# Moving ScalarE's norm chain by one slot in a software-pipelined local-attention stage

## The chip, the cores and the metric

One program on one core of one Trainium2 chip. The metric is device time in microseconds of that core; smaller is better.

## The reference, cut to what matters

The model is a stack of four pairs of cross-attention and feed-forward on x of shape (4, 256, 128). The first feed-forward slot holds six *local layers*, and these fill most of the time. Each local layer is, for every one of the 4 batch rows and for 16 heads of 64:

```python
qkv = shift_tokens(x) @ Wqkv;  q, k, v = split(qkv)
q = l2norm(q) * q_scale;  k = l2norm(k) * k_scale      # t / max(|t|, 1e-12) per head
q, k = rotary(q), rotary(k)
sim = einsum('bhwie,bhwje->bhwij', q, look(k)) * 8      # windows of 32, each with the one before it
out = softmax(mask(sim)) @ look(v);  x = out @ Wo + x
x = ffn(shift_tokens(x)) + x                            # LayerNorm, W1, a * gelu(gate), W2
```

The change concerns `l2norm`: the sums of squares of a unit's query and key per head, and from them 1/|t|.

## The kernel before, in words

All of it is float32. The six local layers are cut into 96 *units*: 6 layers x 4 batch rows x 2 blocks of 128 tokens x 2 halves of 8 heads (`unit_of`). The loop over `LOCAL_SLOTS` (96) is written once for every engine (`pe_local`, `act_local`, `dve_local`, `pool_local`, and the unit loop of `sync_program`), each with its own hand-written order of calls inside a slot. The engines meet only through semaphores that count units. A slot s works on several units at once, by the lags `TURN, SCORE, SOFT, VALUE, OUT = 2, 3, 4, 5, 6`. The LayerNorm and feed-forward of a finished batch row (`ended(slot, lag)`) are spread over slots by lags from 10 to 15, so there are four kinds of slot, by s mod 4.

**TensorE in slot s**, in order (line of the matmul): query of unit s (L721), transposes of the rotated query of s-2 (L750), output projection of s-6 (L822), with s mod 4 = 0 the gate products (L662, L663), value of s (L741), key of s (L730), with s mod 4 = 2 the LayerNorm centring (L255), transposes of the weights of s-5 (L791), scores of s-3 (L780, 64 small matmuls), weighted values of s-5 (L807, 64 small matmuls), feed-forward parts (L265, L671, L679 to L688), transposes of the rotated key of s-2 (L758), and with s mod 4 = 2 the last feed-forward product (L697). `pe_weighted` (L807) waits first for `p_kept` of unit s-5. `pe_turn_query` waits for `k_kept` of the unit before, as both use one bank.

**ScalarE in slot s** (`act_local`): with s mod 4 = 3 the LayerNorm Ln and Exp (L270, L272); squares of the query of s (L1875); Exp of the scores of s-4 (L1920); last gate (L1958); copy of the turned query of s-2 (L1896); copy of the value of s (L1889); squares of the key of s (L1882); copy of the turned weights of s-5 (L1927, sets `p_kept`); gates (L1951, L1952), LayerNorm squares (L260), Gelu with its two table loads (L1965 to L1967, s mod 4 = 1); copy of the turned key of s-2 (L1905); copy of the weighted values of s-5 (L1935); and last `act_norm` of unit s (L1911, L1913, L1915: Relu, Ln and Exp over 128x16, each waiting for the one before), which waits for `summed` of unit s.

**VectorE in slot s** (`dve_local`): residual of s-6 (L2899, L2900), the three rotary products of the query of s (L2858 to L2860, after its squares), sum and reciprocal of the weights of s-4 (L2888, L2890), the three products of the key (after its squares), mask and maximum of s-3 (L2880, L2882), and last `dve_norm`: the two sums of squares of unit s (L2867, L2868), which set `summed`.

**GpSimd in slot s** (`pool_local`): normalise the weights of s-5 (L4001), add of the key of s-1 (L3975), multiply the query of s-1 by the norms (L3982, waits for `norm_done` of s-1), with s mod 4 = 3 a LayerNorm scale (L4007), add of the query of s (L3970), lower the scores of s-3 by their maximum (L3995), multiply the key of s-1 by the norms (L3989), and in the last slot of a layer the rotary tables of the next (L643).

The norms of unit s lie in one of four buffers (`local_small[u % 4]`), the sums in the same place. The queue of SyncE carries the value windows and the weights and has no norm in it.

```python
def pe_weighted(e, s, m, u):
    e.wait_ge(s["p_kept"], u + 1)
def pool_norm_query(e, s, m, u):
    e.wait_ge(s["norm_done"], u + 1)
```

Of the kernel before, what the change touches and what calls it, by code (L numbers as in the profile page):

```python
# [212 lines left out]
UNITS = DEPTH * B * LAYER_UNITS  # L213
# [16 lines left out]
def ended(slot, lag):  # L230
    lb, rest = divmod(slot - lag, LAYER_UNITS)
    return lb if rest == 0 and 0 <= lb < DEPTH * B else None
# [14 lines left out]
def ln_views(buf):  # L247
    return buf[:, 0:N], buf[:, N:2 * N]
# [9 lines left out]
def act_ln_square(e, s, i, views, bank):  # L258
    e.wait_ge(s["ln_centred"], i + 1)
    e.activation(views[0], bank[:, 0:N], ACT.Square).then_inc(s["ln_squared"], 1)  # L260
# [7 lines left out]
def act_ln_rstd(e, s, i, views, bank, eps):  # L268
    e.wait_ge(s["ln_var"], i + 1)
    e.activation(views[1], bank[:, N:2 * N], ACT.Ln, bias=eps).then_inc(s["ln_logged"], 1)  # L270
    e.wait_ge(s["ln_logged"], i + 1)
    e.activation(views[1], views[1], ACT.Exp, scale=-0.5).then_inc(s["ln_rstd"], 1)  # L272
# [434 lines left out]
def live(u):  # L707
    return 0 <= u < UNITS
# [1162 lines left out]
def act_square_query(e, s, m, u):  # L1871
    e.wait_ge(s["q_made"], u + 1)
    if u >= 2:
        e.wait_ge(s["summed"], u - 1)
    e.activation(m.sq_q[u % 2], m.bank[QB], ACT.Square).then_inc(s["q_squared"], 1)  # L1875


def act_square_key(e, s, m, u):
    e.wait_ge(s["k_made"], u + 1)
    if u >= 2:  # L1880
        e.wait_ge(s["summed"], u - 1)
    e.activation(m.sq_k[u % 2], m.bank[KB], ACT.Square).then_inc(s["k_squared"], 1)  # L1882


def act_value(e, s, m, u):
    e.wait_ge(s["v_made"], u + 1)
    if u >= 4:
        e.wait_ge(s["v64_even"] if u % 2 == 0 else s["v64_odd"], windows_loaded(u - 2))
    e.activation(m.vt[u % 4], m.bank[VB], ACT.Copy).then_inc(s["v_kept"], 1)  # L1889


def act_query(e, s, m, u):
    e.wait_ge(s["q_turned"], u + 1)
    if u >= 2:
        e.wait_ge(s["scored"], u - 1)
    e.activation(m.qT[u % 2], m.bank[TB], ACT.Copy).then_inc(s["q_kept"], 1)  # L1896


def act_key(e, s, m, u):
    lb, stage, b, t, half = unit_of(u)  # L1900
    kT = split(m.kT[(lb % 2) * 2 + half], UP)[:, :, PAD + t * P:PAD + (t + 1) * P]
    if u == 0:
        e.wait_ge(s["zeros_ready"], 1)
    e.wait_ge(s["k_turned"], u + 1)
    e.activation(kT, split(m.bank[TB], UP), ACT.Copy).then_inc(s["k_kept"], 1)  # L1905


def act_norm(e, s, m, u):
    norm = m.local_small[u % 4][:, 0:16]
    e.wait_ge(s["summed"], u + 1)  # L1910
    e.activation(norm, norm, ACT.Relu, bias=m.minus_floor).then_inc(s["norm_logged"], 1)  # L1911
    e.wait_ge(s["norm_logged"], 2 * u + 1)
    e.activation(norm, norm, ACT.Ln, bias=m.floor).then_inc(s["norm_logged"], 1)  # L1913
    e.wait_ge(s["norm_logged"], 2 * u + 2)
    e.activation(norm, norm, ACT.Exp, scale=-0.5).then_inc(s["norm_done"], 1)  # L1915


def act_exp(e, s, m, u):
    e.wait_ge(s["lowered"], u + 1)
    e.activation(m.e[u % ES], m.e[u % ES], ACT.Exp).then_inc(s["exped"], 1)  # L1920


def act_weights(e, s, m, u):
    e.wait_ge(s["p_turned"], u + 1)
    if u >= 2:
        e.wait_ge(s["o_made"], u - 1)
    e.activation(m.pT[u % 2], m.bank[PB], ACT.Copy).then_inc(s["p_kept"], 1)  # L1927


def act_out(e, s, m, u):  # L1930
    e.wait_ge(s["o_made"], u + 1)
    if u >= 2:
        e.wait_ge(s["y_made"], u - 1)
    outs = split(m.banks[:, VB * BANK:(PB + 1) * BANK], 2)[:, :, 0:N]
    e.activation(split(m.oT[u % 2], 2), outs, ACT.Copy).then_inc(s["o_kept"], 1)  # L1935


def act_ln_start(e, s, m, lb):
    act_ln_square(e, s, ln_of_local(lb), ln_views(m.ln_local), m.bank[FB])


def act_ln_end(e, s, m, lb):
    act_ln_rstd(e, s, ln_of_local(lb), ln_views(m.ln_local), m.bank[FB], m.eps)


def act_gates(e, s, m, lb):
    b1 = m.W(home_of(lb)[0], "b1")
    e.wait_ge(s["gate01_made"], lb + 1)
    if lb:
        e.wait_ge(s["a2_done"], lb)  # L1950
    e.activation(m.gate[:, 0:N], m.bank[FB][:, 0:N], ACT.Identity, bias=b1[:, 3:4])  # L1951
    e.activation(m.gate[:, N:2 * N], m.bank[FB][:, N:2 * N], ACT.Identity, bias=b1[:, 4:5]).then_inc(s["gate01_kept"], 1)  # L1952


def act_last_gate(e, s, m, lb):
    rows = FFC[2][1]
    e.wait_ge(s["gate2_made"], lb + 1)
    e.activation(m.gate[0:rows, 2 * N:3 * N], m.bank[FB][0:rows, 0:N], ACT.Identity,  # L1958
                 bias=m.W(home_of(lb)[0], "b1")[0:rows, 5:6]).then_inc(s["gate2_kept"], 1)


def act_gelu(e, s, m, lb):
    rows = FFC[2][1]
    e.wait_ge(s["gate2_kept"], lb + 1)
    e.activation(m.gate[:, 0:2 * N], m.gate[:, 0:2 * N], ACT.Gelu)  # L1965
    e.activation(m.gate[0:rows, 2 * N:3 * N], m.gate[0:rows, 2 * N:3 * N], ACT.Gelu).then_inc(s["gelued"], 1)
    e.preload_act_table_set("natural_log_exp_and_others")  # L1967


def act_local(e, s, m):  # L1970
    for slot in range(LOCAL_SLOTS):
        if ended(slot, RSTD) is not None:
            act_ln_end(e, s, m, ended(slot, RSTD))
        if live(slot):
            act_square_query(e, s, m, slot)
        if live(slot - SOFT):
            act_exp(e, s, m, slot - SOFT)
        if ended(slot, KEEP2) is not None:
            act_last_gate(e, s, m, ended(slot, KEEP2))
        if live(slot - TURN):  # L1980
            act_query(e, s, m, slot - TURN)
        if live(slot):
            act_value(e, s, m, slot)
            act_square_key(e, s, m, slot)
        if live(slot - VALUE):
            act_weights(e, s, m, slot - VALUE)
        if ended(slot, KEEP) is not None:
            act_gates(e, s, m, ended(slot, KEEP))
        if ended(slot, SQUARE) is not None:
            act_ln_start(e, s, m, ended(slot, SQUARE))  # L1990
        if ended(slot, GELU) is not None:
            act_gelu(e, s, m, ended(slot, GELU))
        if live(slot - TURN):
            act_key(e, s, m, slot - TURN)
        if live(slot - VALUE):
            act_out(e, s, m, slot - VALUE)
        if live(slot):
            act_norm(e, s, m, slot)
        if slot == 0:
            act_ln_square(e, s, 2 * B - 1, ln_views(m.ln_local), m.bank[FB])  # L2000
        if slot == 1:
            act_ln_rstd(e, s, 2 * B - 1, ln_views(m.ln_local), m.bank[FB], m.eps)
# [2431 lines left out]
def build(nc, x_in, ctx_in, gates_in, const_in, packs_in, out):  # L4434
    with ExitStack() as stack:
# [10 lines left out]
        @block.scalar  # L4446
        def _(e):
            act_cross0(e, s, m)
            act_local(e, s, m)
            act_drain(e, s, m)  # L4450
# [147 lines left out]
```

## Time and profile before

| | us |
|---|---|
| three runs | 1290.18, 1287.36, 1283.38 |
| their median | 1287.36 |
| the profiled execution's own time | 1283.86 |
| its span, first to last instruction | 1282.1 |
| local stage: first L721 to last L721 | 177.2 to 970.8 |
| busy over the span: PE, DVE, ACT, POOL | 95%, 77%, 73%, 61% |

The profiled execution is some 3.5 us below the median of the three. The span is 1.8 us shorter than its time. The stage of the 96 slots takes from 177 to about 978 us, some 8.35 us a slot. The mean granted TensorE clock over the span is 0.990 of full speed. A row of a timeline gives start, duration, engine and line; a bracket at its end is the engine's idle time before it and what ended that. ScalarE, VectorE and TensorE overlap the end of one instruction with the start of the next, so an instruction's cost in a full queue is the distance from its start to the next start, not its duration.

### The profile page before, as it was taken

What the parts mean: (1) busy time and instruction counts of PE and PEld (TensorE: products, weight loads), DVE (VectorE), ACT (ScalarE), POOL (GpSimd) and SP (SyncE); (2) the same over time, 40 slices, a digit from 0 to 9 for tenths busy, and PEclk for the clock granted to TensorE, in tenths of its full rate; (3) what the DMA queues carried; (4) which work ended last, traced back from release to release, by engine and by line L of the source; (5) the groups of instructions that cost most, each with busy time, mean ns of one, the idle gap of its engine ahead of it and who ended that gap; (6) DMA issues with size and microseconds to landing.
All of it is one profiled execution on the core that took longest, in us unless ns stands there. A gap on an engine that the chain in (4) does not pass through costs nothing.

```text
span 1282.1 us, 44796 instructions
## 1 busy us (share of the span) xinstructions
PE 1214.4 (95%) x17900; PEld 870.4 (68%) x17900; DVE 986.0 (77%) x2513; ACT 937.0 (73%) x2310; POOL 786.2 (61%) x805
## 2 busy tenths in 40 slices
PE   7999988999999999999999999999999999999997
PEld 5777745666766677667777677667777877777553
DVE  4666668887887888878888788888888655778677
ACT  6777765677776777777777777777777768788891
POOL 3444447878876877778778777887776102635100
PEclk9999999999999999999999999999999989999998
DMA  5000032222223322342225222432232002213000
GB/s 213 1 2 1 2 116 72 68 63 57 62 62 101 100 64 62 81 125 59 59 62 146 60 61 63 123 84 65 63 81 60 2 1 87 81 35 91 2 1 17
DMA packets 71743, 81.89 MB, mean 64 GB/s; under 512 B 15456, under 2 KB 63584, under 8 KB 71024
## 3 DMA queue, kind: packets, MB, share of 16 engines
q1 hardware_dynamic: 71536, 79.03, 22.4%
q8 instruction: 143, 2.34, 0.8%
q14 instruction: 64, 0.52, 0.1%
HBM read 31.22 MB, written 0.56 MB: 25 GB/s over the span
## 4 chain that ended last, share of the span: by engine, by line
PE 50%; ACT 18%; DVE 17%; issue 10%; POOL 5%; DMA 1%; SPq 0%; ACTq 0%; DVEq 0%; POOLq 0%
PE banks L822 3%; PE banks L807 3%; PE banks L390 2%; PE banks L730 2%; PE banks L741 2%; PE banks L721 2%; ACT arena L2183 2%; PE banks L1142 2%; DVE arena L2858 2%; PE banks L750 2%; PE banks L1136 2%; PE banks L419 2%; DVE arena L2859 2%; DVE small L2867 2%; PE banks L404 2%
## 5 line engine op out<-in xcount | busy, mean ns | idle before, releaser
L3995 POOL TENSOR_TENSOR arena<-arena,small 128x512 f32<-128x512 f32 x93 | 97.1, 1044 | 139.2 <-DVE small L2882 139.2
L1905 ACT ACTIVATE arena<-banks 128x512 f32<-128x512 f32 x94 | 56.2, 598 | 142.3 <-PE banks L758 142.1
L2858 DVE TENSOR_TENSOR arena<-banks,rotary 128x512 f32<-128x512 f32 x192 | 131.6, 685 | 26.8 <-ACT arena L1875 15.9
L3970 POOL TENSOR_TENSOR arena<-arena 128x512 f32<-128x512 f32 x96 | 122.9, 1280 | 30.4 <-DVE arena L2860 30.3
L807 PE MATMUL banks<-arena 64*64 64x32 f32 x5824 | 107.3, 220 | 17.8 <-issue 11.5
L3975 POOL TENSOR_TENSOR arena<-arena 128x512 f32<-128x512 f32 x95 | 121.5, 1279 | 0.2 <-DVE arena L2860 0.2
L606 POOL TENSOR_TENSOR arena<-arena,small 128x512 f32<-128x512 f32 x64 | 66.6, 1041 | 89.0 <-DVE small L533 89.0
L807 PEld LDWEIGHTS banks<-arena 64*64 64x64 f32 x5824 | 95.5, 134 | 29.3 <-issue 12.5
L721 PE MATMUL banks<-slot,z 128*128 128x512 f32 x192 | 100.2, 604 | 3.0 <-DVE arena L2860 1.9
L3982 POOL TENSOR_TENSOR arena<-arena,small 128x512 f32<-128x512 f32 x95 | 99.7, 1049 | 1.3 <-ACT small L1915 1.3
L3989 POOL TENSOR_TENSOR arena<-arena,small 128x512 f32<-128x512 f32 x95 | 99.2, 1044 | 0.0
L741 PE MATMUL banks<-slot,z 128*128 128x512 f32 x192 | 99.0, 598 | 0.0
L730 PE MATMUL banks<-slot,z 128*128 128x512 f32 x192 | 98.0, 592 | 0.0
L822 PE MATMUL banks<-arena,slot 128*128 128x128 f32 x720 | 97.4, 278 | 0.0
L4001 POOL TENSOR_TENSOR arena<-arena,small 128x512 f32<-128x512 f32 x91 | 95.0, 1044 | 0.0
L460 ACT ACTIVATE arena<-arena,small 128x256 f32<-128x256 f32 x128 | 63.7, 500 | 39.7 <-DVE small L565 39.7
L750 PEld LDWEIGHTS banks<-constants,arena 128*128 128x128 f32 x376 | 42.3, 142 | 69.8 <-issue 69.0
L822 PEld LDWEIGHTS banks<-arena,slot 128*128 128x128 f32 x720 | 87.3, 191 | 0.5
L2899 DVE TENSOR_TENSOR z<-z,banks 64x128 f32<-64x128 f32 x90 | 25.0, 277 | 77.4 <-PE banks L822 77.3
L780 PE MATMUL banks<-arena 64*32 64x64 f32 x5952 | 80.9, 224 | 0.5 <-issue 0.5
L2860 DVE TENSOR_TENSOR arena<-banks,rotary 128x256 f32<-128x256 f32 x192 | 79.3, 413 | 0.0
L2859 DVE TENSOR_TENSOR arena<-banks,rotary 128x256 f32<-128x256 f32 x192 | 79.3, 413 | 0.0
(403 smaller groups left out, 3366.3 us busy)
## 6 DMA issues: line engine op xcount, KB each, us to landing
arena<-arena SPq DMA_DIRECT2D x576, 64.0 KB
slot<-in_pack_dram SPq DMA_DIRECT2D x28, 339.5 KB, 3.6
arena<-arena SPq DMA_DIRECT2D x288, 32.0 KB
slot<-in_pack_dram SPq DMA_DIRECT2D x2, 2713.5 KB, 9.1
slot<-in_pack_dram SPq DMA_DIRECT2D x1, 2693.5 KB
slot<-in_pack_dram SPq DMA_DIRECT2D x1, 2316.5 KB
arena<-gate_store SPq DMA_DIRECT2D x8, 256.0 KB, 4.0
slot<-in_pack_dram SPq DMA_DIRECT2D x4, 337.0 KB, 4.3
```

Source lines behind the costliest of these rows:

```text
L721: e.matmul(m.bank[QB], m.zs[b][:, t * P:(t + 1) * P], m.W(stage, "Wqkv")[:, half * BANK:(half + 1) * BANK], start=True, stop=True, skip_gr ...
L730: e.matmul(m.bank[KB], m.zs[b][:, t * P:(t + 1) * P], m.W(stage, "Wqkv")[:, at:at + BANK], start=True, stop=True, skip_group_check=True).t ...
L741: e.matmul(m.bank[VB], m.zs[b][:, t * P:(t + 1) * P], m.W(stage, "Wqkv")[:, at:at + BANK], start=True, stop=True, skip_group_check=True).t ...
L807: made = e.matmul(m.bank[PB if x else VB][y * DH:(y + 1) * DH, to:to + WINDOW], v[rows, i, k, :], pT[rows, at:at + WINDOW], start=True, st ...
L822: made = e.matmul(m.bank[S0][:, N:N + P], wo[:, c * D:(c + 1) * D], oT[:, k * P:(k + 1) * P], start=(k == 0), stop=(k == UP - 1), skip_gro ...
L2858: e.tensor_tensor(rot, made, cos, ALU.mult)
L2859: e.tensor_tensor(sinp[:, :, 0:mid], made[:, :, mid:DH], sin[:, :, 0:mid], ALU.mult)
L3970: e.tensor_tensor(m.rot_q[u % ROTS], m.rot_q[u % ROTS], m.sin_q[u % 2], ALU.add).then_inc(s["q_added"], 1)
L3975: e.tensor_tensor(m.rot_k[u % ROTS], m.rot_k[u % ROTS], m.sin_k[u % 2], ALU.add).then_inc(s["k_added"], 1)
L3982: e.tensor_tensor(q, q, stretch(m.local_small[u % 4][:, 0:UH], DH), ALU.mult).then_inc(s["q_rotated"], 1)
L3989: e.tensor_tensor(k, k, stretch(m.local_small[u % 4][:, UH:2 * UH], DH), ALU.mult).then_inc(s["k_rotated"], 1)
L3995: e.tensor_tensor(p, p, stretch(m.local_small[u % 4][:, 16:24], SPAN), ALU.subtract).then_inc(s["lowered"], 1)
```

## The change

`act_norm` of a unit moves from the end of its own slot to the middle of the next slot, right behind the squares of that slot's key and ahead of the copy of the turned weights. Slot 95 has it in both places, for unit 94 in the middle and for unit 95 at the end. No instruction, wait or buffer is added or removed.

```diff
@@ -1982,6 +1982,8 @@
         if live(slot):
             act_value(e, s, m, slot)
             act_square_key(e, s, m, slot)
+            if slot:
+                act_norm(e, s, m, slot - 1)
         if live(slot - VALUE):
             act_weights(e, s, m, slot - VALUE)
         if ended(slot, KEEP) is not None:
@@ -1994,7 +1996,7 @@
             act_key(e, s, m, slot - TURN)
         if live(slot - VALUE):
             act_out(e, s, m, slot - VALUE)
-        if live(slot):
+        if slot == UNITS - 1:
             act_norm(e, s, m, slot)
         if slot == 0:
             act_ln_square(e, s, 2 * B - 1, ln_views(m.ln_local), m.bank[FB])
```

## Rows read from the trace of the kernel before

**Rows 1.** Busy time of PE, PEld, DVE, ACT, POOL: slots 59-62; whole stage

```profile
664.61:698.57 33.96, 32.89 (x640) 23.86 (x639) 28.23 (x63) 25.34 (x54) 26.77 (x26) 1.00 0.44 122
...
sum 793.00, PE 756.22 PEld 541.19 DVE 656.48 ACT 580.76 POOL 629.39; mean PE 94.53 PEld 67.65 DVE 82.06 ACT 72.59 POOL 78.67
```

**Rows 2.** Waits in the stage, 177 to 970 us: total, times, longest

```profile
ACT arena L1905 <- PE banks L758: 139.7, 73, 4.3
...
ACT small L1911 <- DVE small L2868: 42.1, 50, 3.5
...
PE banks L807 <- issue: 11.5, 15, 2.1
...
PE banks L807 <- ACT arena L1927: 6.0, 19, 0.6
```

**Rows 3.** Timeline of slot 59 (s mod 4 = 3)

```profile
664.28 0.68 DVE L2868 TENSOR_REDUCE small<-arena 128x8 f32<-128x512 f32 x1
...
664.99 0.31 ACT L1911 ACTIVATE small<-small,eps 128x16 f32<-128x16 f32 x1 [0.39 <-DVE small L2868]
...
665.67 0.21 ACT L1915 ACTIVATE small<-small 128x16 f32<-128x16 f32 x1
665.79 0.46 ACT L270 ACTIVATE arena<-banks,eps 128x256 f32<-128x256 f32 x1
...
667.66 1.02 PE L730 MATMUL banks<-slot,z 128*128 128x512 f32 x2
...
668.08 1.05 POOL L3982 TENSOR_TENSOR arena<-arena,small 128x512 f32<-128x512 f32 x1
...
668.52 0.60 PE L791 MATMUL banks<-constants,arena 128*128 128x128 f32 x4
...
668.72 0.60 ACT L1882 ACTIVATE arena<-banks 128x512 f32<-128x512 f32 x1
...
669.05 0.86 PE L780 MATMUL banks<-arena 64*32 64x64 f32 x64
...
669.21 0.59 ACT L1927 ACTIVATE arena<-banks 128x512 f32<-128x512 f32 x1
...
669.86 1.14 PE L807 MATMUL banks<-arena 64*64 64x32 f32 x64
```

**Rows 4.** Timeline of slot 69 (s mod 4 = 1)

```profile
752.98 1.02 PE L730 MATMUL banks<-slot,z 128*128 128x512 f32 x2
...
754.27 0.60 ACT L1882 ACTIVATE arena<-banks 128x512 f32<-128x512 f32 x1
...
755.40 1.14 PE L807 MATMUL banks<-arena 64*64 64x32 f32 x64 [0.18 <-ACT arena L1927]
```

**Rows 5.** Timeline of slot 62 (s mod 4 = 2)

```profile
692.58 1.02 PE L730 MATMUL banks<-slot,z 128*128 128x512 f32 x2
...
694.50 0.60 ACT L1927 ACTIVATE arena<-banks 128x512 f32<-128x512 f32 x1 [0.27 <-PE banks L791]
...
695.23 1.13 PE L807 MATMUL banks<-arena 64*64 64x32 f32 x64
```

**Rows 6.** Timeline of the fill: norms of units 0, 4; slot 6

```profile
183.20 0.31 ACT L1911 ACTIVATE small<-small,eps 128x16 f32<-128x16 f32 x1 [2.67 <-DVE small L2868]
...
209.13 0.31 ACT L1911 ACTIVATE small<-small,eps 128x16 f32<-128x16 f32 x1 [3.54 <-DVE small L2868]
...
215.46 1.02 PE L721 MATMUL banks<-slot,z 128*128 128x512 f32 x2
```

**Rows 7.** Timeline of TensorE: a wait in slot 16, a stall in slot 28

```profile
300.37 0.66 PE L791 MATMUL banks<-constants,arena 128*128 128x128 f32 x4 [1.12 <-POOL arena L4001]
...
405.53 0.54 PE L807 MATMUL banks<-arena 64*64 64x32 f32 x22 [2.06 <-issue]
```

**Rows 8.** Busy times, clock (before the last two): slot 16; behind slot 28

```profile
299.00:304.00 5.00, 3.88 (x140) 3.13 (x140) 4.58 (x10) 2.23 (x6) 4.79 (x6) 1.00 0.26 63
...
407.30:410.50 3.20, 3.20 (x14) 2.01 (x13) 0.00 (x0) 2.84 (x8) 2.77 (x3) 0.59 0.77 237
```

## The prediction

> **What bounds the kernel now.** I read the busy times by stretch first, then the waits of the local stage, then the timelines of single slots. The busy times show an almost full TensorE: 32.89 of 33.96 us in four typical slots, 756 of 793 us in the stage, with ScalarE at 25.3 and GpSimd at 26.8 us of the same 33.96 [rows 1]. So TensorE's 37 us of idle time are all that an edit of the other engines can win there. The waits show why the edit looks attractive: in 50 slots ScalarE stood before the norms for the sums of squares, 42.1 us in all [rows 2]. But its largest wait, 139.7 us, is for TensorE's turned keys, so time saved ahead of that is mostly waited again. The reader is to look next at what TensorE waits for: on ScalarE's copy of the weights (L1927) it waited 6.0 us in 19 slots, the figure to watch, as that copy is what the edit puts the norms in front of.
>
> The timeline of slot 59 shows how tight it is [rows 3]. TensorE's key product (L730) ends at 668.68, ScalarE squares the key from 668.72, copies the weights from 669.21 to 669.80, and TensorE begins the weighted values (L807) at 669.86. Meanwhile TensorE has the turning of the weights and the scores, from 668.52 on; the scores' last start falls just before 669.86. The cover is used up to 0.06 us: nothing can go between the squares and the weights' copy without TensorE waiting for it.
>
> **The change, part by part.** *Price of a norm in ScalarE's queue.* Start to start from the Relu (664.99) to the instruction behind the Exp (665.79) it is 0.80 us [rows 3]. The count of instructions stays, so nothing is paid for work, only for place. The Trainium skill ("ScalarE: Activation LUTs", Rules for kernel authors) budgets about 0.3 us per ACTIVATE and 0.83 ns per element, an estimate of 0.94 us for three over 16 elements; by it the steady sum would be about 12 us larger. The row's start-to-start time is for this very triple and I use it alone.
>
> *Norms of s-1 between squares and weights' copy.* The sums of unit s-1 end with the slot before (664.96 for a slot whose key squares come at 668.72, [rows 3]), so the norms start at once. From L730's end to L807's start it will take 0.04 + 0.49 + 0.80 + 0.59 + 0.06 = 1.98 us in every slot, as the squares cannot start before L730 ends on the same TensorE. What it takes now differs by kind of slot. s mod 4 = 3: 1.18 us, so +0.80 [rows 3]. s mod 4 = 0: no work stands between L730 and L791 there either, +0.80. s mod 4 = 1: L730 ends at 754.00, L807 starts at 755.40; the squares came 0.23 us late, because ScalarE had entered the slot behind its norms; this lateness goes, +0.58 [rows 4]. s mod 4 = 2: a LayerNorm product stands before the turning of the weights, the copy waited 0.27 us for it, and the gap is 693.60 to 695.23, 1.63 us, so +0.35 [rows 5]. Four slots pay 2.53 us. Weights are copied in slots 5 to 95; the 90 slots from 6 on make 22.5 fours: **+57 us**.
>
> *Exceptions among these.* In slots 7 to 11 the squares come 0.4 to 0.7 us late today, more than in slot 69: -2. In the slots that follow GpSimd's tables, as slot 16, TensorE waits 1.12 us for the normalised weights [rows 7]; the norms fit in that wait and cost nothing: three such slots, and part of it in two more, -3. In slot 95 TensorE waits for something else anyway: -1. **Steady part +51 us.**
>
> *Norms away from the end of the slot.* There ScalarE no longer stands for the sums and enters the next slot up to 0.8 us earlier, or more. In the steady part this gives only the 0.23 us counted above: queries, values and keys arrive when TensorE makes them, and TensorE is late by then. Behind the Gelu with its table loads (s mod 4 = 1) TensorE waits for the turned key; both ends of that chain move with L807, so the wait stays. While the pipeline fills it gives more: in slots 0 to 4 ScalarE stood five times before the norms, 2.67 us at the first and 3.54 at the last [rows 6], and the squares of the next query, its products and the next slot's query came behind. I walked these slots with the new order and the durations of the rows: now GpSimd's multiply by the norms sets them, and slot 6 starts near 209 and not at 215.46: **-6 us**. Its bounds are 0 (another wait takes each one's place) and about -15 (five waits of some 3 us all gone).
>
> *GpSimd.* Its multiply of the query (L3982), at 668.08 in slot 59, will wait for norms that end near 668.72 + 0.49 + 0.68 + 0.21 = 670.10, 2.0 us later. Behind it queue a LayerNorm scale, an add, the lowering of the scores, the other multiply, the normalising of the next weights. GpSimd works 26.8 us in four slots that become 36.5 long, so 2.4 us a slot are idle [rows 1]. Walked through, the next weights are normalised near 676.2 and TensorE turns them near 677.1 at the new pace: 1.0 us of slack, cost 0. The bounds: 0, and 1 us a slot of one kind in four, +24 us. In the slot behind the tables the slack is negative, as today.
>
> *VectorE and queues.* The query's products come earlier, the key's as before. SyncE's queue has no norm in it and no DMA moves: 0. *The stalls called "issue"*, in the midst of L807, total 11.5 us in 15 slots [rows 2]. A TensorE that has just waited may have its next instructions at hand, which would remove up to all of it; but such stalls also stand in slots with a wait before L807, so I count 0 and keep -12 as an end.
>
> **Sum.** +57 - 6 - 6 = +45 us. Against the profiled execution's own 1283.86 this is 1328.9; that execution is 3.5 us below the median of the three runs, against which it is 1332.4. I give 1330.
>
> **The rivals.** *Faster, because the norm wait set the period.* The loop is sums, norms, squares of the next query, its products. If L807 did not really hang on L1927, the 42.1 us of waiting before the norms would fall out, as far as TensorE's 37 us of idle time allow: 1283.9 - 37 = 1247. For it speaks that the chain of waits of the page runs over DVE and ACT for a third of the span; against it, that TensorE hardly idles and L807 starts 0.06 us behind the copy. It would decide only if the copy had 0.8 us of slack. *No difference:* if TensorE's scores really end 0.8 us later than the modelled ends say, the delay would hide and the time stay near 1284. *The instruction stalls vanish:* 1330 - 12 = 1318. *GpSimd becomes the bound,* behind its later multiply: 1330 + 24 = 1354.
>
> *The clock falls.* Behind the 2.06 us stall in slot 28 [rows 7] the granted clock was 0.59 for 3.2 us, that is, partly 1.2 instead of 2.4 GHz; behind the 1.12 us wait of slot 16 it stayed at 1.00 [rows 8]. The new waits are 0.35 to 0.8 us, shorter than both, so I expect no fall. If one came per four slots at slot 28's price, 3.2 x 0.41 = 1.3 us, it would add 24 x 1.3 = 31 us: 1361. The Trainium skill ("TensorE: Matmul & The Clock Gate", A second HAM failure mode) says that frequent short idle times between groups of matmuls can make the clock swing; by that rule the edit would cost more than its waits, while slot 16's row so far speaks against it.
>
> **How the numbers follow.** The forecast 0.78; stalls vanish 0.08; GpSimd bound 0.04; clock 0.05; faster 0.03; no difference 0.02. About 0.5% is what a measurement of this kernel can tell from no change. Faster 0.03, same 0.02, slower 0.95. The range takes in the fill's bounds (-9 and +6 around 1330), the vanished stalls (1318) and a few us of slack lost on GpSimd: 1315 to 1346.
>
> **What would show it.** Right: in every steady slot L1882, L1911, L1913, L1915, L1927 in one row, L807 starting 0.06 us behind L1927's end with a wait on it of 0.35 to 0.8 us, some 50 to 57 us over the stage in the waits where there were 6.0; the wait of L1911 for L2868 gone; slot 6 starting near 209; stage longer by about 45 us, everything after unchanged. Wrong: L807 without a wait; TensorE waiting for L3982 or L4001 in ordinary slots; a granted clock below 1.00 in typical slots; or slot 6 still near 215.

## The result, and the profile after

The changed kernel takes 1318.69 us (median of six runs, 1316.82 to 1321.41) against 1285.12 us (the kernel before, six runs, 1281.63 to 1290.18): ratio 1.026, 95% interval 1.024 to 1.028. It is slower by some 34 us; 45 were forecast, and the time lies inside the stated range. The profiled execution took 1317.78 us, with a span of 1316.0.

The waits of the stage after, 177 to 1000 us: each row has what waited and for what, then the total in us, how often, and the longest. A wait called `issue` is one for which the profile shows no semaphore. `L3984` is GpSimd's multiply of the query (L3982 before; lines behind the edit shift by two), the other lines are those of before.

```profile
POOL arena L3984 <- ACT small L1915: 178.8, 88, 3.2
ACT arena L1905 <- PE banks L758: 125.5, 68, 3.4
...
ACT arena L1889 <- PE banks L741: 62.1, 92, 1.5
PE banks L807 <- ACT arena L1927: 53.3, 85, 1.0
...
PE banks L750 <- POOL arena L3984: 4.2, 4, 2.2
PE banks L791 <- POOL arena L4003: 3.8, 6, 0.8
...
PE banks L807 <- issue: 2.9, 4, 1.6
```

Read against [rows 2], three things moved. ScalarE's wait for the sums of squares, 42.1 us in the stage before, is not among them any more. TensorE's wait at L807 for the weights' copy rose from 6.0 to 53.3 us. And the stalls called issue in L807 fell from 11.5 to 2.9 us. ScalarE did not save its 42.1 us: it now stands 62.1 us for TensorE's value product (L741), which was 3.5 us before. The largest wait, GpSimd's for the norms, is new and costs nothing in the ordinary slots: TensorE's wait for GpSimd at L791 is 3.8 us, no more than before:

```profile
PE banks L791 <- POOL arena L4001: 4.5, 4, 1.5
...
ACT arena L1889 <- PE banks L741: 3.5, 8, 0.7
```

Its four waits at L750, 4.2 us, all lie in slots 2 to 5, while the pipeline fills.

The timeline of slot 59 after, the same slot as in [rows 3] (start, duration, engine and line; the bracket is idle time before it):

```profile
683.54 1.02 PE L730 MATMUL banks<-slot,z 128*128 128x512 f32 x2
...
684.60 0.60 ACT L1882 ACTIVATE arena<-banks 128x512 f32<-128x512 f32 x1 [0.26 <-PE banks L730]
...
684.93 0.86 PE L780 MATMUL banks<-arena 64*32 64x64 f32 x64
685.09 0.30 ACT L1911 ACTIVATE small<-small,eps 128x16 f32<-128x16 f32 x1
685.42 0.31 ACT L1913 ACTIVATE small<-small,eps 128x16 f32<-128x16 f32 x1
...
685.76 0.22 ACT L1915 ACTIVATE small<-small 128x16 f32<-128x16 f32 x1
...
685.88 0.58 ACT L1927 ACTIVATE arena<-banks 128x512 f32<-128x512 f32 x1
686.05 1.04 POOL L3984 TENSOR_TENSOR arena<-arena,small 128x512 f32<-128x512 f32 x1 [2.41 <-ACT small L1915]
...
686.52 1.14 PE L807 MATMUL banks<-arena 64*64 64x32 f32 x64 [0.73 <-ACT arena L1927]
```

L730 ends at 684.56, L807 starts at 686.52: 1.96 us, where 1.98 was worked out and 1.18 stood before. The norms' place in ScalarE's queue, 685.09 to 685.88, is 0.79 us wide. The scores of L780, which used to end just as the copy did, now end 0.73 us before L807 can start. In the other kinds of slot:

```profile
774.53 1.02 PE L730 MATMUL banks<-slot,z 128*128 128x512 f32 x2
...
777.51 1.13 PE L807 MATMUL banks<-arena 64*64 64x32 f32 x64 [0.73 <-ACT arena L1927]
```

```profile
710.51 1.02 PE L730 MATMUL banks<-slot,z 128*128 128x512 f32 x2
...
713.48 0.73 PE L807 MATMUL banks<-arena 64*64 64x32 f32 x36 [0.29 <-ACT arena L1927]
```

The first is slot 69 (1.96 us from L730's end, 1.40 before), the second slot 62 (1.95 us, 1.63 before). One chain now sets these kinds of slot alike. Slots 59 to 62, and the whole stage (us, then busy PE, PEld, DVE, ACT, POOL, clock, DMA, GB/s):

```profile
680.49:716.82 36.33, 33.04 (x639) 23.82 (x638) 28.56 (x62) 25.77 (x55) 26.68 (x26) 1.00 0.41 113
...
177.00:1004.30 827.30, 755.18 (x14506) 537.84 (x14507) 661.71 (x1434) 589.08 (x1241) 630.37 (x620) 1.00 0.30 77
```

The four slots are 2.37 us longer than before (36.33 against 33.96), where 2.53 was worked out. TensorE does the same work, 755.18 us against 756.22 [rows 1], in a stage some 34 us longer. Its granted clock is 1.00 on average over the stage. The stage's beginning:

```profile
203.47 1.11 PE L750 MATMUL banks<-constants,arena 128*128 128x128 f32 x4 [2.25 <-POOL arena L3984]
...
211.71 0.59 PE L721 MATMUL banks<-slot,z 128*128 128x512 f32 x1
```

Slot 6 starts at 211.71 and not at 215.46 [rows 6]: the fill gave 3.8 us (4.0 counted from each kernel's own first L721, at 177.5 and 177.2).

### The profile page after: what moved, and what is told of

Read it like the earlier page. It is cut to its first block, busy times and chain, and to the rows that moved or that the text cites. A ratio compares the mean times of both kernels' runs of the same rounds, so it can differ in the third digit from the quotient of the medians.

```text
span 1316.0 us, 44796 instructions
## 1 busy us (share of the span) xinstructions
PE 1214.0 (92%) x17900; PEld 866.4 (66%) x17900; DVE 990.4 (75%) x2513; ACT 945.3 (72%) x2310; POOL 786.0 (60%) x805
## 4 chain that ended last, share of the span: by engine, by line
PE 66%; ACT 21%; issue 4%; DVE 4%; POOL 3%; SPq 1%; DMA 1%; ACTq 0%; DVEq 0%; POOLq 0%
PE banks L822 6%; PE banks L807 6%; PE banks L730 6%; PE banks L741 6%; PE banks L721 4%; ACT arena L1882 4%; ACT arena L1927 4%; PE banks L750 3%; PE banks L758 2%; PE banks L390 2%; ACT small L1913 2%; PE banks L697 2%; ACT L1965 2%; PE banks L1142 2%; PE banks L1136 2%
## 5 line engine op out<-in xcount | busy, mean ns | idle before, releaser
L3984 POOL TENSOR_TENSOR arena<-arena,small 128x512 f32<-128x512 f32 x95 | 99.2, 1044 | 184.0 <-ACT small L1915 184.0
L807 PE MATMUL banks<-arena 64*64 64x32 f32 x5824 | 104.5, 220 | 57.1 <-ACT arena L1927 54.1
L1905 ACT ACTIVATE arena<-banks 128x512 f32<-128x512 f32 x94 | 56.1, 597 | 129.6 <-PE banks L758 129.4
L807 PEld LDWEIGHTS banks<-arena 64*64 64x64 f32 x5824 | 93.9, 134 | 72.0 <-ACT arena L1927 68.2
L3997 POOL TENSOR_TENSOR arena<-arena,small 128x512 f32<-128x512 f32 x93 | 97.2, 1046 | 12.1 <-DVE small L2884 11.9
L1889 ACT ACTIVATE arena<-banks 128x512 f32<-128x512 f32 x96 | 57.4, 598 | 64.5 <-PE banks L741 62.7
L721 PE MATMUL banks<-slot,z 128*128 128x512 f32 x192 | 98.5, 594 | 0.9 <-DVE arena L2862 0.9
L741 PE MATMUL banks<-slot,z 128*128 128x512 f32 x192 | 99.1, 598 | 0.0
L730 PE MATMUL banks<-slot,z 128*128 128x512 f32 x192 | 98.4, 594 | 0.0
L750 PEld LDWEIGHTS banks<-constants,arena 128*128 128x128 f32 x376 | 41.3, 141 | 76.4 <-issue 68.8
L780 PE MATMUL banks<-arena 64*32 64x64 f32 x5952 | 80.1, 224 | 0.2 <-issue 0.2
L2862 DVE TENSOR_TENSOR arena<-banks,rotary 128x256 f32<-128x256 f32 x192 | 79.6, 414 | 0.0
```

Of the source, the lines that this page charges most:

```text
L721: e.matmul(m.bank[QB], m.zs[b][:, t * P:(t + 1) * P], m.W(stage, "Wqkv")[:, half * BANK:(half + 1) * BANK], start=True, stop=True, skip_gr ...
L730: e.matmul(m.bank[KB], m.zs[b][:, t * P:(t + 1) * P], m.W(stage, "Wqkv")[:, at:at + BANK], start=True, stop=True, skip_group_check=True).t ...
L741: e.matmul(m.bank[VB], m.zs[b][:, t * P:(t + 1) * P], m.W(stage, "Wqkv")[:, at:at + BANK], start=True, stop=True, skip_group_check=True).t ...
L807: made = e.matmul(m.bank[PB if x else VB][y * DH:(y + 1) * DH, to:to + WINDOW], v[rows, i, k, :], pT[rows, at:at + WINDOW], start=True, st ...
L3984: e.tensor_tensor(q, q, stretch(m.local_small[u % 4][:, 0:UH], DH), ALU.mult).then_inc(s["q_rotated"], 1)
L3997: e.tensor_tensor(p, p, stretch(m.local_small[u % 4][:, 16:24], SPAN), ALU.subtract).then_inc(s["lowered"], 1)
```

## The experiments

All ratios are to the kernel before, run on the same chip in the same session. Its median differs between the sessions, so the ratios are to be compared, and not the times across sessions; each interval is that of the ratio. Every kernel was profiled once.

| kernel | median us (runs) | before, same session | ratio, 95% interval | L807 waits for copy, us | L807 issue, us |
|---|---|---|---|---|---|
| before | 1285.12 (6) | | 1 | 6.0 | 11.5 |
| the change | 1318.69 (6) | 1285.12 | 1.026 (1.024 to 1.028) | 53.3 | 2.9 |
| norms behind the weights' copy | 1309.42 (4) | 1283.89 | 1.019 (1.014 to 1.024) | none | 12.1 |
| norms ahead of the value's copy | 1276.21 (8) | 1283.89 | 0.994 (0.991 to 0.997) | 0.4 | 13.1 |
| the same again | 1277.12 (6) | 1287.72 | 0.990 (0.988 to 0.993) | 0.4 | 12.0 |
| norms ahead of the Exp | 1276.63 (6) | 1287.72 | 0.992 (0.989 to 0.995) | 0.4 | 11.2 |
| norms ahead of the key's squares | 1292.17 (10) | 1283.89 | 1.005 (1.003 to 1.007) | 22.8 | 3.5 |
| before + three activations | 1322.94 (4) | 1283.89 | 1.030 (1.025 to 1.035) | 54.7 | 0.9 |
| before + one activation | 1289.56 (10) | 1287.94 | 1.001 (0.998 to 1.003) | 8.3 | 8.7 |
| before + three, at the turned key | 1332.54 (4) | 1287.94 | 1.034 (1.031 to 1.037) | 1.1 (at L750: 52.8) | 11.7 |
| change from unit 6 on | 1319.60 (4) | 1287.94 | 1.024 (1.021 to 1.027) | 51.9 | 2.9 |
| change up to unit 4 | 1279.83 (6) | 1287.94 | 0.993 (0.990 to 0.996) | 6.2 | 12.0 |

The two columns at the right are the rows "PE banks L807" of each kernel's waits, 177 to 1000 us; "none" means that there is no such row. They list single waits of some 0.2 us and more.

**Norms behind the weights' copy.** The edit to the changed kernel:

```diff
-            if slot:
-                act_norm(e, s, m, slot - 1)
         if live(slot - VALUE):
             act_weights(e, s, m, slot - VALUE)
+        if slot:
+            act_norm(e, s, m, slot - 1)
```

> Norms of s-1 one place later than in the change: behind the copy of the weights (L1927), ahead of gates and Gelu. Theory (TensorE hangs on the weights' copy, the norms' 0.80 us in front of it are the whole loss): the wait of L807 for that copy falls to nearly nothing, 49 us come back. Instead the key's copy behind the Gelu comes 0.8 us later in one slot of four and L750 waits for it, 22 x 0.8 = +18 us; lateness of the squares in one slot of four goes, -5; fill -4; the stalls called issue return to some 11 us. Time about 1285 + 18 - 5 - 4 = 1294. Rival (what costs is that the norms come a slot later at all, so that GpSimd's multiply is late): the time stays near 1319 or rises, since the norms here end 0.5 us later still.

Measured: 1309.42 us. The wait at L807 is gone, as the theory says, so it is the copy of the weights that the norms must not stand before. But the time is 15 us above what I expected. Its waits show most of why:

```profile
PEld banks L791 <- POOL arena L4003: 39.2, 45, 2.9
...
PE banks L750 <- ACT arena L1905: 18.2, 17, 1.1
...
PE banks L791 <- POOL arena L4003: 11.9, 10, 2.1
...
PE banks L671 <- ACT arena L1952: 6.6, 19, 0.6
```

Beside the wait for L1905 behind the Gelu that I had named (18.2 us, 5.1 before), TensorE waits at L671 for the gates, which in slots with s mod 4 = 0 now stand behind the norms, and at L791 for GpSimd's normalising: 11.9 us against 4.5. Most of this stands in the fill (1.86 us) and in four slots behind GpSimd's tables (some 2.1 us each). The 45 waits of the weight load there (PEld, 39.2 us) show that the slack is used up in ordinary slots as well. Further, the granted clock was some 0.5 in three stretches of this trace's stage (0.52 at 310.0 to 313.4, 0.50 at 689.0 to 695.8 and at 726.6 to 730.0); in the changed kernel such a fall stands only in the fill. So the rival, late norms through GpSimd, is real at this place, if small; at the place of the change the ordinary slots do not show it.

**Norms ahead of the value's copy.**

```diff
         if live(slot):
+            if slot:
+                act_norm(e, s, m, slot - 1)
             act_value(e, s, m, slot)
             act_square_key(e, s, m, slot)
-            if slot:
-                act_norm(e, s, m, slot - 1)
```

> Norms of s-1 ahead of the copy of the value of s, where ScalarE stands 0.6 us a slot for TensorE's value product in the changed kernel. Theory: neither squares of the key nor weights' copy are delayed, and ScalarE no longer stands for the sums at the end of a slot: L807 waits below 5 us in all, lateness of the squares goes (22 x 0.23 = -5 us), fill -4 to -6: about 1275, faster than both. Rival (the later norms themselves cost, through GpSimd or through ScalarE entering the value late): not faster than 1285; a rival half-way is that Exp and last gate push the value, and with it the squares, by up to 0.4 us in some slots: about 1290.

> The kernel with the norms of s-1 ahead of the copy of the value of s once more, in more rounds and beside the one with the norms ahead of the Exp. Theory: fill -4 and lateness of the squares in one slot of four -5, with the stalls called issue as before: ratio 0.992 to 0.996. Rival (the first comparison was luck of the instruction stalls): 0.997 to 1.000.

Measured: ratio 0.994 and 0.990, both intervals below 1. It is faster than both kernels: 8 and 11 us below the kernel before, a little more than I expected in the second session. The timeline of its slot 59:

```profile
659.82 0.31 ACT L1911 ACTIVATE small<-small,eps 128x16 f32<-128x16 f32 x1
...
660.32 1.02 PE L730 MATMUL banks<-slot,z 128*128 128x512 f32 x2
...
660.62 0.58 ACT L1889 ACTIVATE arena<-banks 128x512 f32<-128x512 f32 x1
...
661.37 0.60 ACT L1882 ACTIVATE arena<-banks 128x512 f32<-128x512 f32 x1 [0.17 <-PE banks L730]
...
661.87 0.59 ACT L1927 ACTIVATE arena<-banks 128x512 f32<-128x512 f32 x1
...
662.51 1.13 PE L807 MATMUL banks<-arena 64*64 64x32 f32 x64
```

The same three activations, also a slot late, stand where ScalarE would wait for TensorE's value product. From L730's end (661.34) to L807 it is 1.17 us again. "A slot later" costs next to nothing (TensorE's wait at L791 is 6.2 us against 4.5); the place is what costs. The gain is in the trace too: the 6.0 us of waiting at L807 are down to 0.4, and slot 6 starts at 212.50 and not at 215.46, together some 8 us.

**Norms ahead of the Exp.** The same two lines directly behind `act_square_query`.

> Norms of s-1 one place further ahead than in front of the value: directly behind the squares of the query of s, ahead of the Exp of the scores, for which ScalarE stood 11 us in 21 slots with the norms in front of the value. Theory (all places ahead of the value product are free): no wait of L807 for the weights' copy above the 5 us of the kernel with the norms ahead of the value, same time as that within 4 us, ratio to before 0.992 to 0.997. Rival: the Exp 0.8 us later makes VectorE's sums of the weights and with them the normalising late, so L791 waits for L4003: slower than the kernel before by 0.5% or more.

Measured: 0.992, at the lower edge of what the theory says, and the rival is out; its interval overlaps that of the place ahead of the value, so the two are not told apart.

**Norms ahead of the key's squares.** The two lines between `act_value` and `act_square_key`.

> Norms of s-1 between the value's copy and the squares of the key. ScalarE has some 0.37 us to spare there before the key product is done, so theory says the squares come 0.43 us late and the gap from L730's end to L807's start is 1.61 us in each kind of slot, not 1.98: +0.43, +0.43, +0.2, 0 against before by kind, 1.07 per four slots = +24 us; fill -4, stalls called issue about -5: about 1300. Rival (any place in the middle of the slot costs the whole 0.80): 1315 to 1320.

Measured: 1.005, 1292.17 us; 1300 was expected and the rival's 1315 is excluded. TensorE waits 22.8 us at L807. That is 17 us more than before, where the working had 24 more; and the issue stalls fell by 8.0 us to 3.5, where I had allowed 5. These two more than cover the 8 us by which I was too high.

**Three more activations in the kernel before**, nothing moved. They write spare columns and no output depends on them:

```diff
+def act_extra(e, s, m, u):
+    spare = m.local_small[u % 4][:, 40:56]
+    e.activation(spare, m.ident[:, 0:16], ACT.Relu, bias=m.minus_floor).then_inc(s["mask_ready"], 1)
+    e.wait_ge(s["mask_ready"], 3 * u + 3)
+    e.activation(spare, spare, ACT.Ln, bias=m.floor).then_inc(s["mask_ready"], 1)
+    e.wait_ge(s["mask_ready"], 3 * u + 4)
+    e.activation(spare, spare, ACT.Exp, scale=-0.5).then_inc(s["mask_ready"], 1)
...
             act_square_key(e, s, m, slot)
+            act_extra(e, s, m, slot)
```

> The kernel before with three further activations of the norms' size and kinds on spare columns, each waiting for the one before, right behind the squares of the key; the real norms stay at the end of their slot. This pays the insertion without moving anything. Theory: +0.80, +0.80, +0.80, +0.35 by kind of slot, about +60 us, and TensorE's wait before L807 takes the place of the stalls called issue in it, -11: about 1332. Rival A (those stalls are a matter of chance between executions and not of the wait): they stay at some 12 us and the time is about 1343. Rival B (the insertion hides in TensorE's pipeline and the loss of the change came from later norms): within 5 us of 1285.

Measured: 1322.94 us, 1.030. Its waits:

```profile
PE banks L807 <- ACT arena L1936: 54.7, 89, 1.2
...
PE banks L807 <- issue: 0.9, 2, 0.7
```

This pays the insertion alone, and it pays what the change pays (L1936 is the weights' copy here): 39 us, where the change costs 34 with some 4 gained in the fill. Rival B is out, and rival A as well: the stalls fell from 11.5 to 0.9 us. The time is 9 us below the theory's 1332, because the listed waits grew by 49 us and not by 60.

**One more activation.** Only the first of the three, no wait behind it.

> A smaller dose than the three extra activations: one extra Relu of 128x16 behind the squares of the key, no wait behind it. I expect a pitch of 0.2 to 0.34 us. Theory: TensorE waits that much before L807 in three kinds of slot of four and nothing in the kind that had 0.27 us to spare: 0.2 x 3 x 22.5 = +13 to +23 us; the stalls called issue in L807 fall part of the way, from 14 to some 8 us, -6. Time 1291 to 1301. Rival (the stalls do not depend on the wait): they stay near 14 us, time up to 1307.

Measured: 1289.56 us, ratio 1.001. I had expected 7 to 17 us more than the kernel before; it is 1.6, and the interval ends at 4. The pitch is small, as its timeline shows:

```profile
672.93 0.30 ACT L1920 ACTIVATE small<-constants,eps 128x16 f32<-128x16 f32 x1
673.13 0.59 ACT L1932 ACTIVATE arena<-banks 128x512 f32<-128x512 f32 x1
```

0.20 us a slot raises the wait at L807 by 2.3 us in the rows (waits of under about 0.2 us are mostly not listed) and takes 2.8 us off the stalls. The profiled execution, 1293.04 us, is the slowest of its ten, so its stage is no measure of the median; that a small insertion is nearly free is what the interval says, not how it divides.

**Three more, at the turned key.** The same function in front of `act_key`, behind a wait for `k_turned`.

> The three extra activations at another place: in front of the copy of the turned key, behind its wait, so that TensorE waits some 0.8 us before L750 in three kinds of slot of four and not before L807. +0.8 x 3 x 22.5 = +54 us by the copy. Theory A (any wait of TensorE lets its next instructions arrive): the stalls called issue in L807 fall to a few us, time about 1284 + 54 - 10 = 1328. Theory B (only a wait just before the two blocks of 64 small matmuls helps): they stay at 12 to 15 us, time about 1340.

Measured: 1332.54 us. Its waits:

```profile
PE banks L750 <- ACT arena L1905: 52.8, 67, 1.1
...
PE banks L807 <- issue: 11.7, 14, 2.2
```

TensorE waits just as long in all, 52.8 us, but at the start of the slot, and the stalls in L807 stay at 11.7 us: theory B. The wait must stand shortly before the small matmuls. The time is 45 us above the kernel before, where theory B gives 56 and theory A 44. By the time alone it would be theory A; the rows decide against it: the waits at L750 grew by 48 us and not by the 54 that both theories count, and the stalls did not fall.

**The change in parts.** From unit 6 on (`if slot >= 7` for the new place, `if slot < 6 or slot == UNITS - 1` for the old), and up to unit 4 (`if 1 <= slot <= 5` and `if slot >= 5`).

> The change only from unit 6 on: units 0 to 5 have their norms at the end of their own slot as before, later units behind the next key's squares. Theory (steady part and fill add up): slot 6 starts near 215.5 us as before, the rest as in the changed kernel, so 1318.7 + 4.3 = 1323. Rival (the fill gives nothing that lasts): 1319.

> The reverse: units 0 to 4 have their norms behind the next key's squares, from unit 5 on at the end of their own slot as before. Theory: slot 6 starts some 4 us earlier and the rest is as before: 0.3% below the kernel before, about 1280 against 1284. Rival: the gain of the fill is taken back by slot 12, ratio 1.000.

Measured: 1.024 for the steady part, 0.993 for the fill alone. The first gives 1319.60 us, where the theory said 1323 and its rival 1319; its interval, 1.021 to 1.027, holds the 1.026 of the whole change and not the 1.029 that 1323 would be. So the times speak for the rival. The traces of the stage speak for the theory. First the kernel with the steady part alone, then the whole change, with the first and the last start of L721:

```profile
L721 PE MATMUL banks<-slot,z x192: 590/592/1062, 177.1 to 1008.6; 128*128 128x512 f32 x192
...
L721 PE MATMUL banks<-slot,z x192: 590/592/697, 177.5 to 1004.8; 128*128 128x512 f32 x192
```

Slot 6 starts at 215.92 and 211.71, and from there to the last L721 it is 792.7 and 793.1 us: the 4 us of the fill are still there at the end of the stage. What follows the stage is 1.5 us shorter in this execution, and the kernel before had a median of 1287.94 us beside this one and of 1285.12 beside the whole change: the times are too rough for 4 us.

The fill alone starts slot 6 at 211.15, 4.3 us earlier than before. Its median is 8 us lower, about twice that, and the interval leaves out the 0.997 that 4 us would be as well as the rival's 1.000. In its one trace only 0.6 us of the 4.3 are left at the last L721 (970.2 against 970.8), and the granted clock explains part of that: it fell three times in the stage behind slot 6 (0.50 in the two stretches below and from 429.2 to 432.6), where the kernel before has the one fall of [rows 8].

```profile
241.50:244.90 3.40, 3.40 (x11) 2.21 (x12) 0.93 (x2) 2.34 (x7) 3.40 (x4) 0.50 0.40 102
...
712.50:715.90 3.40, 3.40 (x23) 2.24 (x20) 1.13 (x2) 1.02 (x3) 3.38 (x4) 0.50 0.23 56
```

So the fill gives some 4 us; how much of the 8 us is its doing stays open.

## Why the prediction was right, and which term was off

The forecast was +45 us and the time grew by 34. The mechanism held; of the terms, one was sized at nothing that is 8 to 9 us, and a smaller one was too large.

*The price of a norm in the queue:* 0.80 us worked out, 0.79 measured. The estimate of 0.94 us, worked out from the budget of the Trainium skill ("ScalarE: Activation LUTs", Rules for kernel authors), would have been too high for this triple; the measurement decides.

*The gap from L730 to L807:* 1.98 us foreseen for every kind of slot, 1.95 to 1.96 found in all three kinds shown. The steady part, +57 with -6 of exceptions, was +51; summed over the timelines of slots 6 to 95, the gap is 50.2 us longer. The listed waits at L807 rose by 53.3 - 6.0 = 47.3 us, 1.0 of it in slot 5. That ScalarE's 42.1 us of waiting before would not come back, because TensorE had been nearly full, was right: no gain beyond the fill shows in the stage.

*The fill:* -6 forecast, -3.8 found. That GpSimd's multiply by the norms would set these slots is borne out: before L750 TensorE waits for it in slots 2 to 5, 2.25 us at the last. Behind that wait TensorE ran slower, as the timeline row and the stretch from 203.4 us show:

```profile
204.38 1.91 PE L741 MATMUL banks<-slot,z 128*128 128x512 f32 x2
...
203.40:207.40 4.00, 3.93 (x8) 1.92 (x8) 3.93 (x9) 1.11 (x2) 4.00 (x5) 0.57 0.28 69
```

L741 took 1.91 us where it takes 1.02 at full speed, and the granted clock of the stretch was 0.57, partly 1.2 instead of 2.4 GHz. I had counted such a fall for no slot. But it is not what is missing: the kernel with the change up to unit 4 has the same order of calls up to here and no such fall, and its slot 6 starts at 211.15, 0.6 us sooner and still 2 us behind the 209 of the forecast. There TensorE waits 1.85 us for GpSimd's normalising of the first weights, which it reached late in the changed kernel (0.23 us of waiting), and then for their copy:

```profile
207.45 0.66 PE L791 MATMUL banks<-constants,arena 128*128 128x128 f32 x4 [1.85 <-POOL arena L4003]
...
209.59 1.14 PE L807 MATMUL banks<-arena 64*64 64x32 f32 x64 [0.65 <-ACT arena L1927]
```

The forecast named neither wait.

*The stalls called issue:* this is the term that failed. I counted 0 "since such stalls also stand in slots with a wait before L807" and kept -12 as an end. They fell by 8.6 us in the change. The waits I had pointed to were some 0.2 to 0.5 us; at 0.2 us the stalls are still 8.7, at 0.36 us 3.5, at 0.73 us 2.9 and 0.9. So the rival given 0.08 was true beside the forecast and not instead of it; its 1318 is nearer to the measured time than the 1330 forecast, which the range still covers. The sum with measured terms, +47.3 - 8.6 - 3.8 = +34.9, meets the 33.9 by which the span grew (1282.1 to 1316.0). That it meets so well is partly luck: the gaps grew by 50.2 and not by 47.3 us, the 1.0 us of slot 5 is in both the waits and the fill, and the slow stretch behind slot 28's stall [rows 8], at 0.41 x 3.2 = 1.3 us, is gone with that stall.

*GpSimd and the clock:* no cost in the steady part, as forecast. The slack of about 1.0 us on GpSimd was real: in slot 60 of the changed kernel the next weights are normalised at 691.89 and TensorE turns them at 692.99, and one place later, half a microsecond more, the waits at L791 appeared. TensorE's granted clock stayed at 1.00 from slot 6 on with a wait of 0.3 to 0.7 us in every slot, so what the Trainium skill reports of another kernel ("TensorE: Matmul & The Clock Gate", A second HAM failure mode), that frequent short idle times make it swing, did not happen here at these lengths.

*The rival on the other side,* faster by 37 us, failed on the condition named for it: the copy of the weights had no slack.

## What to carry to other kernels

When an instruction is moved off one engine's wait, look at who waits for what comes behind its new place: here 0.8 us of ScalarE before a copy that TensorE takes with 0.06 us to spare cost 0.35 to 0.8 us in every slot. One place ahead, before the squares, they still cost 0.5% in all; two places ahead and further, before the copy of the value or the Exp, they cost nothing and let the whole kernel gain 0.6 to 1.0%. Work out the gap between two events of the full engine along the other engine's queue, kind of slot by kind of slot. A long wait on an engine that is not the bound is no gain in store.

## What the runs showed of the hardware that was not expected

TensorE's stalls that no semaphore explains, in the midst of a block of 64 small matmuls, depend on what TensorE did just before. With no wait before L807, or only the few of the kernel before, they total 11.2 to 13.1 us over the stage in six traces of five kernels; with a wait of 0.6 to 0.7 us in front of it 0.9 to 2.9 us in three kernels; with one of 0.8 us in front of L750, some 5 us earlier in the slot, 11.7 us.

The traces also show what these stalls wait for: instructions. The profile lists, apart from the data, a DMA queue of kind `instruction`; its queue 8 has 143 packets of 16 KB in every trace. In the stage of all twelve traces L807 stops in mid-block for more than 0.15 us 118 times, and always at the same 18 of its 5824 matmuls. At each of these places it is the same packet, counted from the start, that landed last, and L807 goes on 1.2 to 1.6 us after its landing (once after 0.9). Of all matmuls of the stage before, only 6% start 1.1 to 1.7 us behind a packet. Slot 28 before, with the row of the packet from the DMA view of 403.2 to 403.3 us, in which it starts:

```profile
402.60 0.88 PE L807 MATMUL banks<-arena 64*64 64x32 f32 x42
...
405.53 0.54 PE L807 MATMUL banks<-arena 64*64 64x32 f32 x22 [2.06 <-issue]
```

```profile
q8 instruction: 1, 0.02, 60.1%
```

The last figure is the packet's time as a share of 16 engines' 0.1 us, so it took 0.96 us and landed at about 404.2, 1.3 us before L807 went on. In the changed kernel the same packet starts at 403.4, hardly later, but L807 of slot 28 only at 408.36, and runs through:

```profile
408.36 1.14 PE L807 MATMUL banks<-arena 64*64 64x32 f32 x64 [0.73 <-ACT arena L1927]
```
Over the 18 places the packet starts 1.0 us ahead of its block in the kernel before (median), 2.0 us in the changed one, and 0.9 us with the wait in front of L750. So in these stalls TensorE waits for late instructions, and a wait just before the block gives them time to arrive. What decides when a packet starts no view shows.

The spread of the runs does not follow as clearly: the three kernels with the long wait before L807 ran 1316.82 to 1325.83 over 14 runs, each within 5 us, and the kernel before 1278.09 to 1289.59 in one session of 17 runs; but the kernel with the norms ahead of the key's squares, whose stalls are down to 3.5 us, spread over 10 us in its 10 runs.
